# Expert attention on one Trainium2 core: a unit's scores, maxima, exponentials and transposes in two parts, and two stage handovers moved

## What is computed

```python
logits = x @ router_w + router_b
_, top2 = jax.lax.top_k(jax.nn.softmax(logits, -1), 2)
for e in range(4):                      # the reference orders the members first; the result is the same
    q, k, v = ...                       # xg @ wq[e] + bq[e] and so on, 16 heads of 8
    att = jnp.einsum('bqhd,bkhd->bhqk', q, k) * 0.5
    att = jnp.where(valid[:, None, None, :], att, -1e9)
    att = jax.nn.softmax(att, axis=-1)
    y = jnp.einsum('bhqk,bkhd->bqhd', att, v).reshape(b, s, d) @ wo[e] + bo[e]
    out = out + w_tok[..., None] * y
```

## Time and profile before

| what | value |
|---|---|
| median of 3 runs | 1204.99 us (1204.27 to 1205.66) |
| the profiled execution | 1205.75 us |
| its span in the profile | 1203.9 us |
| TensorE (PE) busy | 1036.5 us |
| VectorE (DVE) busy | 753.6 us |
| ScalarE (ACT) busy | 549.6 us |
| GpSimd (POOL) busy | 447.1 us |
| expert loop, first score to first wide mask | 431.3 to 687.0 us |
| wide attention | to about 836 us |

### The profile page before, as it was taken

The page is one execution under the profiler, slowest core; times in us unless marked ns, Lnnn a source line. Parts: engine busy times, 40 slices in busy tenths (PEclk is TensorE's granted clock), DMA queues, the critical chain, the costliest instruction groups (busy, mean ns, idle before and its releaser), DMA issues. The chain is left out here.

```text
span 1203.9 us, 30164 instructions
## 1 busy us (share of the span) xinstructions
PE 1036.5 (86%) x12369; PEld 782.5 (65%) x12369; DVE 753.6 (63%) x1475; ACT 549.6 (46%) x1000; POOL 447.1 (37%) x496
## 2 busy tenths in 40 slices
PE   5899999998576679999999989997889958699992
PEld 4788888886454557777777756665436625567771
DVE  2455655554495568888888858886568778631222
ACT  2455555554233246666666635553545424342220
POOL 1132333322245624444444433321324157236142
PEclk9999999999898769999999979997989869889996
DMA  8300050000000100000000000000784110011324
GB/s 246 127 1 1 2 142 2 1 1 1 0 1 1 36 1 2 3 3 3 2 3 2 2 1 2 2 2 2 228 323 124 30 36 3 3 57 55 97 91 126
DMA packets 37943, 53.15 MB, mean 44 GB/s; under 512 B 3024, under 2 KB 29264, under 8 KB 37424
## 3 DMA queue, kind: packets, MB, share of 16 engines
q1 hardware_dynamic: 35824, 46.97, 12.4%
q0 software_dynamic: 1984, 4.26, 1.0%
HBM read 29.08 MB, written 22.14 MB: 43 GB/s over the span
## 5 line engine op out<-in xcount | busy, mean ns | idle before, releaser
L1515 ACT COPY e_PT<-probsT 128x512 f32<-128x512 f32 x192 | 103.5, 589 | 154.8 <-PE probsT L1363 154.8
L1363 PE MATMUL probsT<-W,e_P 128*128 128x128 f32 x768 | 106.8, 284 | 15.5 <-ACT e_P L1522 15.5
L505 POOL TENSOR_TENSOR c_P<-c_P,c_rl 128x1024 f32<-128x1024 f32 x32 | 60.7, 1896 | 127.7 <-DVE c_rl L645 127.7
L1522 ACT ACTIVATE e_P<-e_P 128x1024 f32<-128x1024 f32 x96 | 102.7, 1070 | 5.6 <-DVE e_P L1620 4.0
L1363 PEld LDWEIGHTS probsT<-W,e_P 128*128 128x128 f32 x768 | 86.8, 144 | 19.1 <-ACT e_P L1522 17.7
L1617 DVE TENSOR_REDUCE e_mx<-scores 128x16 f32<-128x1024 f32 x64 | 78.4, 1225 | 30.6 <-PE scores L1351 29.3
L642 DVE TENSOR_REDUCE c_rl<-c_P 128x8 f32<-128x1024 f32 x32 | 39.0, 1220 | 81.9 <-ACT c_P L329 81.9
L542 PEld LDWEIGHTS misc<-c_xs,c_AQ 128*128 128x128 f32 x488 | 62.2, 194 | 35.0 <-issue 33.4
L1190 POOL TENSOR_TENSOR e_RK<-e_Ks,W 128x512 f32<-128x512 f32 x64 | 65.9, 1039 | 51.2 <-PE scores L1351 28.3
L1620 DVE TENSOR_TENSOR e_P<-scores,e_mx 128x1024 f32<-128x1024 f32 x64 | 78.4, 1225 | 6.5
L1376 PEld LDWEIGHTS mixed<-e_Vbd,e_PT 128*64 128x64 f32 x2048 | 64.9, 138 | 26.1 <-issue 19.3
(11 more groups left out here) (366 smaller groups left out, 2345.7 us busy)
## 6 DMA issues: line engine op xcount, KB each, us to landing
hbm_dist<-u_Z SPq DMA_DIRECT2D x16, 768.0 KB, 8.4
u_S<-hbm_dist SPq DMA_DIRECT2D x64, 128.0 KB, 2.8
e_w<-in_w SPq DMA_DIRECT2D x12, 256.0 KB, 2.8
W<-in_wpack SPq DMA_DIRECT2D x1, 2489.0 KB, 13.1
hbm_slots<-c_blank SPq DMA_DIRECT2D x6, 350.0 KB, 6.2
e_xin<-hbm_slots SPq DMA_DIRECT2D x6, 350.0 KB, 3.4
W<-in_wpack SPq DMA_DIRECT2D x1, 2048.0 KB, 8.7
hbm_results<-c_blank SPq DMA_DIRECT2D x1, 2048.0 KB, 11.5
```

Of the source, the lines that this page charges most:

```text
L505: pool.tensor_tensor(pr, pr, bc(rl[:, a.up, :].unsqueeze(2), [P, PAIRS, KEYS]), ALU.mult).then_inc(s["scaled"], 1)
L1363: last = pe.transpose(K.psT[:, i * P:(i + 1) * P], Pr[:, n % 2, i * P:(i + 1) * P], K.ident)
L1515: act.copy(PT[:, n % 2, half * 512:(half + 1) * 512], K.psT[:, half * 512:(half + 1) * 512]).then_inc(s["tcopied"], 1)
L1522: act.activation(Pr[:, n % 2, :], Pr[:, n % 2, :], ACT.Exp, scale=0.5 if n < TOTAL else CSCALE).then_inc(s["exped"], 1)
```

## The change

1. Expert loop: `score` is called twice a unit, for row groups 0 and 1 ahead of mixing and for row groups 2 and 3 behind it. Part one waits for and signals semaphores of its own (`shiftedA`, `scoredA`, `maxedA`). `shift` takes maxima and differences of 512 columns, part by part.
2. The exponential is two instructions of 512 columns, each with its signal, and the four transposes of a half wait for their half alone; so also in the wide, the relative and the causal attention (there behind one subtraction of 1024 columns).
3. POOL spreads the wide attention's keys and copies its values for tiles 0 and 1 at n = 59 and n = 60.
4. `next_norm` gives VectorE and POOL the statistics and factors of the relative attention's norm: groups 0 to 2 inside the wide attention, group 3 after the relative attention's first normalisation. The constants come first on POOL.

```diff
+def next_norm(K):
+    s = K.sems(K.es, "n5_", "stats var vareps rstd normed turned copied")
+    st6, mv, rstd = K.rows5
+    K.n5 = s, mv, rstd
+    def stats(dve, g, written):
+        if written is not None:
+            dve.wait_ge(written, 4 * (g + 1))
+        for t in range(4 * g, 4 * g + 4):
+            last = dve.bn_stats(st6[:, t, :], K.X[:, t, :])
+        last.then_inc(s["stats"], 1)
+        dve.wait_ge(s["stats"], g + 1)
+        for t in range(4 * g, 4 * g + 4):
+            last = dve.bn_aggr(mv[:, t, :], st6[:, t, :])
+        last.then_inc(s["var"], 1)
+    def scale(pool, g):
...
+    K.next_stats, K.next_scale = stats, scale
...
-                        if n == TOTAL:
+                        if n == TOTAL - 5:
                             wide_keys(0)
                             pool.wait_ge(c["ones"], 1)
                             wide_values(0)
+                        if n == TOTAL - 4:
+                            wide_keys(1)
+                            wide_values(1)
...
                     for t in range(TILES):
-                        wide_keys(t + 1)
-                        wide_values(t + 1)
+                        if t:
+                            wide_keys(t + 1)
+                            wide_values(t + 1)
                         if t % 4 == 1:
                             rows_scale(t // 4 + 1)
+                        if t >= 6 and t % 4 == 2:
+                            K.next_scale(pool, t // 4 - 1)
...
-                    def score(n):
-                        if n >= TOTAL:
-                            return
+                    def score(n, part):
                         t, e = divmod(n, U)
-                        wait(pe, s["shifted"], n)
+                        wait(pe, s["shifted" if part else "shiftedA"], n)
                         pe.wait_ge(s["qout"], t + 1)
                         pe.wait_ge(s["kbd"], n + 1)
-                        tiles = [(r, b, slice(32 * r, 32 * r + 32), slice(64 * b, 64 * b + 64)) for b in range(TB) for r in range(4)]
+                        tiles = [(r, b, slice(32 * r, 32 * r + 32), slice(64 * b, 64 * b + 64)) for b in range(TB)
+                                 for r in (2 * part, 2 * part + 1)]
...
-                        last.then_inc(s["scored"], 1)
+                        last.then_inc(s["scored" if part else "scoredA"], 1)
...
-                        pe.wait_ge(s["exped"], n + 1)
                         for half in range(2):
+                            pe.wait_ge(s["exped"], 2 * n + half + 1)
                             wait(pe, s["tcopied"], 2 * (n - 1) + half + 1)
...
-                        score(n + 1) if n + 1 < TOTAL else wide_score(0)
+                        if n + 1 < TOTAL:
+                            score(n + 1, 0)
                         mix(n - 1)
+                        score(n + 1, 1) if n + 1 < TOTAL else wide_score(0)
                         turn(n)
...
-                        act.wait_ge(s["shifted"], n + 1)
-                        act.activation(Pr[:, n % 2, :], Pr[:, n % 2, :], ACT.Exp, scale=0.5 if n < TOTAL else CSCALE).then_inc(
-                            s["exped"], 1)
+                        for half in range(2):
+                            act.wait_ge(s["shiftedA" if n < TOTAL and half == 0 else "shifted"], n + 1)
+                            cols = slice(half * 512, (half + 1) * 512)
+                            act.activation(Pr[:, n % 2, cols], Pr[:, n % 2, cols], ACT.Exp, scale=0.5 if n < TOTAL else CSCALE).then_inc(s["exped"], 1)
...
+                        for part, tag in enumerate(("A", "")):
+                            rows = slice(2 * part, 2 * part + 2)
+                            sc = K.ps4[:, rows, 0:256].rearrange("p r (h k) -> p r h k", h=4)
+                            pr = Pr[:, n % 2, part * 512:(part + 1) * 512].rearrange("p (r h k) -> p r h k", r=2, h=4)
+                            top = mx[:, n % 2, 8 * part:8 * part + 8].rearrange("p (r h) -> p r h", r=2)
+                            dve.wait_ge(s["scored" + tag], n + 1)
+                            wait(dve, s["shifted" + tag], n - 1)
+                            dve.tensor_reduce(top, sc, AX.X, ALU.max).then_inc(s["maxed" + tag], 1)
+                            wait(dve, s["turned"], 2 * (n - 2) + part + 1)
+                            dve.wait_ge(s["maxed" + tag], n + 1)
+                            dve.tensor_tensor(pr, sc, bc(top.unsqueeze(3), [P, 2, 4, S]), ALU.subtract).then_inc(
+                                s["shifted" + tag], 1)
...
                         if u == 1 and t % G == 0:
                             rows_stats(t // G + 1)
+                        if u == 1 and t % G == 1 and G < t < TILES:
+                            K.next_stats(dve, t // G - 1, c["xsum"])
...
-                for g in range(GROUPS):
-                    rows_stats(g)
                 rows_norm(0)
+                K.next_stats(dve, GROUPS - 1, None)
                 dve.wait_ge(s["biasT"], 2)
```

More of the change, by code:

```diff
@@ L173, in dram @@
             return nc.dram_tensor(name, shape, dt, kind="Internal").ap()
-        shared = dict(nc=nc, A=A, out=out, es=es, early=early, sb=sb, sems=sems, W=W, R=R, X=X, XnT=XnT, ctx=ctx, ctxT=ctxT, nhalf=nhalf, w=w, row=row,
+        shared = dict(nc=nc, A=A, out=out, es=es, early=early, sb=sb, sems=sems, W=W, R=R, X=X, XnT=XnT, ctx=ctx, ctxT=ctxT, nhalf=nhalf, rows5=rows5, w=w, row=row,
                      ident=ident, ps4=ps4, psS=psS, psT=psT, psO=psO, psM=psM, dram=dram)
@@ L1123, in rank_columns @@
     ch.link(dve, dve.tensor_reduce(rank, less[:, :, :, :], AX.X, ALU.add))
+def next_norm(K):
[13 more added lines that the diff above has]
+    def scale(pool, g):
+        tiles = slice(4 * g, 4 * g + 4)
+        pool.wait_ge(s["var"], g + 1)
+        pool.tensor_scalar(rstd[:, tiles], mv[:, tiles, 1], LN_EPS, None, ALU.add).then_inc(s["vareps"], 1)
+        pool.wait_ge(s["vareps"], g + 1)
+        pool.tensor_tensor(rstd[:, tiles], rstd[:, tiles], K.nhalf[:, tiles], ALU.pow).then_inc(s["rstd"], 1)
+    K.next_stats, K.next_scale = stats, scale
 def stage_two_attentions(K):
@@ L1474, in _ @@
                     pe.wait_ge(q["negout"], 1)
-                    score(0)
+                    score(0, 0)
+                    score(0, 1)
                     pe.wait_ge(s["biasout"], 1)
@@ L1931, in turn @@
                         return
-                    pe.wait_ge(s["exped"], t + 1)
                     for half in range(2):
+                        pe.wait_ge(s["exped"], 2 * t + half + 1)
                         wait(pe, s["tcopied"], 2 * (t - 1) + half + 1)
@@ L2029, in exp @@
                     act.wait_ge(s["shifted"], t + 1)
-                    act.activation(Pr[:, t % 2, :], Pr[:, t % 2, :], ACT.Exp, scale=SCALE).then_inc(s["exped"], 1)
+                    for half in range(2):
+                        cols = slice(half * 512, (half + 1) * 512)
+                        act.activation(Pr[:, t % 2, cols], Pr[:, t % 2, cols], ACT.Exp, scale=SCALE).then_inc(s["exped"], 1)
                 def outT(t):
@@ L2058, in values @@
                                           s["vout"], 1)
-                def rows_stats(g):
-                    for t in range(g * GT, (g + 1) * GT):
-                        last = dve.bn_stats(st6[:, t, :], K.X[:, t, :])
-                    last.then_inc(m["stats"], 1)
-                    dve.wait_ge(m["stats"], g + 1)
-                    for t in range(g * GT, (g + 1) * GT):
-                        last = dve.bn_aggr(mv[:, t, :], st6[:, t, :])
-                    last.then_inc(m["var"], 1)
                 def rows_norm(g):
@@ L2394, in exp @@
                     act.wait_ge(s["shifted"], n + 1)
-                    act.activation(Pr[:, n % 2, :], Pr[:, n % 2, :], ACT.Exp, scale=SCALE).then_inc(s["exped"], 1)
+                    for half in range(2):
+                        cols = slice(half * 512, (half + 1) * 512)
+                        act.activation(Pr[:, n % 2, cols], Pr[:, n % 2, cols], ACT.Exp, scale=SCALE).then_inc(s["exped"], 1)
                 def outT(n):
```

27 lines of the change are left out of this document (6 added, 21 removed).

## The result

The changed kernel takes 1226.73 us (median of 5 runs, 1224.07 to 1228.1), the kernel before 1205.66 us beside it (1204.27 to 1206.57): a ratio of 1.0172, 95% interval 1.0158 to 1.0186, slower by 21.1 us where 14.3 were forecast. The profiled execution took 1224.07 us, the shortest of the five, with a span of 1221.9; before, 1205.75 and 1203.9.

What follows compares the result with a forecast made beforehand. The prediction took TensorE's matmul streaming to bound the expert loop. Its terms, +44.2 - 16.5 + 3.0 - 0.5 - 12.3 - 4.2 + 0.6 = +14.3 us, added to 1204.99 gave 1219.3 us, range 1206 to 1229.

Steps and rivals of the forecast that it cites:

- the first seam: Expert loop to wide attention: earlier POOL work removes 5.4 us of TensorE idleness and 6.9 of half clock, -12.3 us.
- Scores in two parts: Expert loop: each half set costs as much as the whole, 0.69 us added per unit over 64 units, +44.2 us.
- the upper bound: Price of half a set of expert scores: from above, 0.68 us plus 0.1 for one more change between array shapes.
- The rival of half sets at half cost: Expert scores: a part costs 0.34 us or runs beside mixing, so TensorE's added time vanishes; 1178 us, chance 0.13.
- The hole of the fourth unit: Expert loop: the transposes' wait for ScalarE's exponential goes, 1.10 us in each of 15 tiles, -16.5 us.
- VectorE: Expert loop: doubled instructions stay hidden on average, but mixing waits 0.2 us a tile for normalising, +3.0 us.
- phase: Expert loop: mixing's wait for normalising queued behind VectorE's second part, taken as 0.2 us a tile.
- Late next is nothing: First seam: once POOL's work is moved, nothing else is late; the spread for wide tile 2 has two units of slack.
- the seam's clock stays low: Rival at the expert-to-wide handover: 1.2 GHz lasts as long as before, +6.9 us, 1226 us, chance 0.08.
- Second seam and statistics: Start of relative attention: transposes start earlier, -4.2 us; statistics inserted on VectorE in the wide attention cost +0.6 us.
- Exponentials: Halves cost ScalarE 0.12 us per unit, hidden; wide, relative and causal pipelines start earlier, about 0.5 us once, -0.5 us.

Runs made afterwards that it cites:

- whole_set: The changed kernel with TensorE's eight masks and eight scores whole again ahead of mixing, VectorE and ScalarE still in halves, both seams as changed: 1190.9 us.
- adjacent: The changed kernel with both parts of a unit's scores issued back to back ahead of mixing: 1186.0 us.
- exp_first: The changed kernel with scores, maxima and subtractions unsplit, and the fourth unit's exponential put ahead of the copies of the next tile's values on ScalarE: 1179.41 us.
- exps: The kernel before with only the exponentials and the transposes' waits in halves, in all four attentions: 1196.11 us.
- unsplit_scores: The changed kernel with scores, maxima and subtractions in one piece, exponentials and transposes in halves, both seams as changed: 1180.51 us, second run 1180.61 us.
- handover1: The kernel before with only POOL's keys and values for wide tiles 0 and 1 moved into the last expert units: 1194.31 us.
- last_tile_2: The changed kernel with both score parts ahead of mixing in the last four expert units, and the first wide score ahead of the last expert mixing: 1219.31 us.
- last_tile: The changed kernel with both score parts ahead of mixing in the last four expert units only: 1224.19 us.
- both_handovers: The kernel before with POOL's wide preparation and the relative attention's statistics both moved earlier, nothing split: 1188.57 us.
- tensore_only: The kernel before with TensorE's scores alone in two parts around mixing, VectorE still working on whole sets: 1331.77 us.

## Why the prediction was right, and where it was not

The forecast case came true in its main term and its sign, and the time lies in the range. In the two traces one term, the first seam, came out nearly 8 us dearer than forecast, and some 5 us that no term had came back elsewhere; so part of the nearness of the forecast is luck. The rival whose mechanism came true had 1226 us, and that its number fits the median of 1226.7 so well is in part luck too.

*Scores in two parts: right.* 0.69 us was added per unit in the forecast. Over six tiles, the time from the first mask of a part to the next kind of work sums to 5.59 us a tile, against 2.71 for the whole sets: 0.72 a unit, including 0.15 us a tile of waiting for VectorE, which the forecast had apart as phase. The comparison of four tiles of 512 columns with eight of 256 was the right one to take. The 0.1 us that the upper bound put on one more change of shape had no row behind it; the parts show at most 0.02 over the 0.68. The rival of half sets at half cost needed a part below 0.47; the parts take 0.66 to 0.70.

*The hole of the fourth unit: right in size.* It is gone, 1.10 us a tile. Halves of the exponential alone leave 9.0 of the 15.5 us, VectorE's halves besides 5.1 (whole_set, and adjacent too), by the groups of their traces. The last 5.1 are gone only in the changed kernel, which differs from adjacent by the split around mixing alone: its unit is 0.7 us longer, and the copies of the values end earlier relative to the transposes, as the step has it. exp_first shows that those copies are what the exponential stood behind.

*VectorE: right.* 0.15 us a tile (0.2 forecast), seen once a tile ahead of mixing, and 14.49 us busy in a tile of 18.11. What the forecast left out: the transposes and the output projection occupy 0.14 and 0.1 us more a tile. Of the 0.14, 0.09 are also in exps and unsplit_scores, where the scores are whole; the rest, and the projection's 0.1, come with the split. The tile came out 2.01 us longer, against 2.76 - 1.10 + 0.2 = 1.86.

*First seam: mis-sized, the step that failed.* "5.4 of idleness, 6.9 of half clock" are what the seam gives alone, 12.3 forecast and 12.8 measured (handover1). In the changed kernel the idle time went and the half clock stayed: 1.2 GHz for 17 us before and after. From the first score of the last tile to the ninth wide mask it took 60.2 us before and 57.9 after, 2.3 less; by the forecast it would have been near 10 less. The sentence that fails is "Late next is nothing": next late was VectorE's normalised output (1.04 us), in the same units in which TensorE had been given the scores in two parts, and with the parts together there and the wide score ahead of mixing (last_tile_2) the clock stays up. The forecast costed the seams and the scores one by one, though its own text said what is queued behind VectorE's second part. The rival "the seam's clock stays low", 1226 us at a chance of 0.08, is what happened; it named the waits only in passing ("TensorE also waits at the last expert units"), and whether they bring the fall is not shown.

*Second seam and statistics: right.* -4.3 us (-4.2 forecast); the insertions cost 0.2 in the run that has them alone.

*Exponentials: sign right, size small.* In the relative attention's start they gave about 0.4 us (0.5 forecast). Behind the seams the changed kernel gained 5.2 us in the relative attention and lost 1.3 later, 3.9 net, which no term had. The table says where it comes from: TensorE's clock was low for 20.4 us of the relative attention before and for 5.6 after, and 14.8 us at half the clock are worth up to 7.4. The changed kernel has the least low clock there of all the traces; in the other kernels with halves it was 10.0 to 15.0 us, so a part of the 5.2 is chance.

So the sum by measured parts of the one execution: +29.7 in fifteen tiles, -2.3 from there to the ninth wide mask, -4.3 at the second seam, and -5.2 for all the rest, which is mostly the relative attention. The score split costs some 40 us (adjacent against the changed kernel, seam clock included). Without the split of scores, maxima and subtractions the rest of the change takes 1180.5 us.

## What to carry to other kernels

Where many small matmuls stand side by side in the array, the price of a set is set by the columns streamed; cutting the set in two and putting a group on all rows between the parts pays those columns twice, while two parts back to back cost 0.09 us here. Splitting work for an earlier start paid here where another engine waits for it (ScalarE's exponential and the transposes), and not on the engine that bounds; and before splitting at all, see whether the late instruction merely stands behind another in its own queue, as the exponential stood behind the copies. When a wait is taken out to keep the clock up, look for the waits that the other edits open in the same stretch: the clock fell beside one that another part of the same change had made. And compare the clock of two traces stretch by stretch before a difference of a few us is put down to an edit.

## What the runs showed of the hardware

- Matmuls on different row groups ran independently of the order in which they were issued: in adjacent the second part's masks started 0.08 us after the first part's and ahead of the first part's scores (rows of 556.85 above).
- The clock fell at the first seam with little idle time on TensorE before it: busy for 10.96 of the 12 us ahead of the fall in the changed kernel, with one wait of 1.04 us in them. Neither figure tells a fall: in whole_set TensorE was busy for 10.03 of the 12 us ahead of the first wide mask, with single waits of 0.32, 0.39 and 1.00 us, and the clock stayed at 2.4 GHz for the 39 us behind. Once down, it stayed at 1.2 GHz for 17 us in the changed kernel and for 7 us in last_tile, under the same kind of work.
- The same wait of 0.81 us for VectorE's output of the wide attention, some 20 us behind its first mask, has a fall of 3.4 us right behind it in handover1, both_handovers, exp_first, last_tile and last_tile_2, and none in adjacent, whole_set, both runs of unsplit scores and the changed kernel. What makes the difference stays open.
- In tensore_only, waits that return in every tile (41 us in sum) took PEclk to 0.86 for a whole tile, with 6.8 us of each steady tile at 1.2 GHz, so that the price of a wait was above its length.
